# Moving GpSimd's weight scaling, a split and four additions in a two-layer network with attention, experts and a state-space scan

## The reference

```
h = layernorm(x) * (1 + ca) + sa;  x = x + ga * attention(h)      # 8 heads, latent keys, causal
h = layernorm(x) * (1 + cb) + sb;  x = x + gb * experts0(h)       # 8 experts of 64, 2 chosen
h = layernorm(x) * (1 + ca) + sa;  x = x + ga * mixer(h)          # state-space scan, 16 states
h = layernorm(x) * (1 + cb) + sb;  x = x + gb * experts1(h)       # 8 experts of 512, 2 chosen
```

```
xr = h @ in_w + in_b;  x_in, res = split(xr);  xc = silu(conv4(x_in))
proj = xc @ x_proj_w + x_proj_b;  d_raw, Bm, Cm = split(proj)
delta = softplus(d_raw @ dt_w + dt_b)
state[n] = exp(delta * A[n]) * state[n] + (delta * xc) * Bm[n]     # over the tokens
y = sum_n state[n] * Cm[n] + xc * D;   out = (y * silu(res)) @ out_w + out_b
```

## Time and profile before

| | us |
|---|---|
| median of 3 runs | 1392.08 (1386.74 to 1392.71) |
| the profiled execution, its own time | 1389.78 |
| its span, first to last instruction | 1388.0 |
| TensorE busy | 1209.2 (87%) |
| VectorE busy | 1064.1 (77%) |
| ScalarE busy | 851.7 (61%) |
| GpSimd busy | 494.3 (36%) |

### The profile page before, as it was taken

One profiled execution on the slowest core, in us unless ns is written; L12 is line 12 of the kernel. 1 busy time (PEld: TensorE's weight loads), 2 busy tenths in 40 slices (PEclk: granted clock), 3 DMA queues, 4 the chain that ended last, 5 costly groups with the idle time before them and its releaser, 6 DMA issues. The chain is left out here.

```text
span 1388.0 us, 19464 instructions
## 1 busy us (share of the span) xinstructions
PE 1209.2 (87%) x6560; PEld 756.6 (55%) x6560; DVE 1064.1 (77%) x2381; ACT 851.7 (61%) x1600; POOL 494.3 (36%) x309
## 2 busy tenths in 40 slices
PE   5974689988898989989899889989899899889698
PEld 4641155655655556545556465655556556555466
DVE  3757976599867997599866998689975998579722
ACT  2624455587647856489565866479565876469332
POOL 0104930087102950068200961049300871039300
PEclk9985579999999999999999999999999999999789
DMA  6102100020001100020001200021000300011000
GB/s 243 70 16 77 46 8 1 21 102 16 16 16 62 61 16 1 16 92 31 16 9 47 85 0 17 16 77 47 16 1 16 108 16 9 1 62 61 8 1 9
DMA packets 18514, 53.22 MB, mean 38 GB/s; under 512 B 4976, under 2 KB 5864, under 8 KB 18032
## 3 DMA queue, kind: packets, MB, share of 16 engines
q1 hardware_dynamic: 16112, 43.40, 9.6%
q0 software_dynamic: 1296, 4.20, 1.0%
q10 hardware_dynamic: 1008, 4.38, 0.8%
HBM read 45.40 MB, written 2.38 MB: 34 GB/s over the span
## 5 line engine op out<-in xcount | busy, mean ns | idle before, releaser
L1456 DVE TENSOR_TENSOR_SCAN probs_T<-bank,probs_T 128x512 f32<-128x512 f32 x256 | 302.8, 1211 | 1.5
L593 PEld LDWEIGHTS bank<-w_w,hidden 128*128 128x128 f32 x2048 | 247.2, 192 | 77.9 <-issue 68.2
L442 POOL TENSOR_TENSOR probs_T<-step_space,probs_T 128x1024 f32<-128x1024 f32 x120 | 285.7, 2387 | 0.4
L577 PE MATMUL bank<-hT,w_w 128*128 128x512 f32 x512 | 256.7, 615 | 10.9 <-ACT hidden L908 10.1
L593 PE MATMUL bank<-w_w,hidden 128*128 128x128 f32 x2048 | 252.2, 276 | 5.2 <-DVE expert_sum L1149 4.1
L440 POOL TENSOR_TENSOR probs_T<-step_space,probs_T 128x512 f32<-128x512 f32 x16 | 25.1, 1571 | 633.9 <-DVE step_space L1443 633.9
L908 ACT ACTIVATE hidden<-bank,w_b 128x512 f32<-128x512 f32 x256 | 169.9, 686 | 112.4 <-PE bank L577 111.8
L981 ACT ACTIVATE probs<-bank,row_neg 128x128 f32<-128x128 f32 (+3 forms) x256 | 135.3, 530 | 165.4 <-DVE row_neg L1310 148.4
L1053 ACT ACTIVATE bank<-step_space,a_neg 128x512 f32<-128x512 f32 x256 | 167.8, 683 | 58.0 <-DVE probs_T L1456 42.4
L676 PE MATMUL bank<-k_pad,q_lat 128*128 128x512 f32 (+3 forms) x512 | 184.8, 447 | 5.4 <-DMA k_pad<-xc 5.4
L1310 DVE TENSOR_REDUCE row_neg<-bank 128x1 f32<-128x128 f32 (+3 forms) x256 | 122.2, 486 | 78.8 <-PE bank L678 76.9
(11 more groups left out here) (183 smaller groups left out, 1603.5 us busy)
## 6 DMA issues: line engine op xcount, KB each, us to landing
probs_T<-b_rows_dram SPq DMA_DIRECT2D x64, 512.0 KB, 3.7
w_w<-in_w_dram ACTq DMA_DIRECT2D x2, 2048.0 KB, 14.0
k_pad<-xc SPq DMA_DIRECT2D x64, 64.0 KB, 2.0
x_in<-in_x_dram POOLq DMA_DIRECT2D x8, 256.0 KB, 3.3
gate<-gate_rows_dram SPq DMA_DIRECT2D x1, 2048.0 KB, 7.0
out_dram<-x_out POOLq DMA_DIRECT2D x7, 256.0 KB, 2.8
step_space<-in_wmod_dram SPq DMA_DIRECT2D x1, 768.0 KB, 5.3
probs_T<-in_wqT_dram SPq DMA_DIRECT2D x1, 512.0 KB, 4.1
```

What stands on the lines that cost most here:

```text
L442: ins = nc.gpsimd.tensor_tensor(inject[:, n % 3, :, :], u[:], row.unsqueeze(1).to_broadcast([P, DH, T]), ALU.mult)
L577: mm(hid1_bank(n)[:], w["w1"][:, n // C1, n % C1 * P:(n % C1 + 1) * P], hT[3][:], start=True, stop=True).then_inc(hid1_mm.sem, 1)
L593: ins = mm(to[:, t * P:(t + 1) * P], hidden[:, (e * C1 + c) % (2 * C1), t * P:(t + 1) * P], w["w2"][:, e * C1 + c, :], start=(c == 0), sto ...
L1456: v.tensor_tensor_scan(state[:, n % 2, c, :], decay(DH * n + c)[:], inject[:, n % 3, c, :], 0.0, ALU.mult, ALU.add).then_inc(st_ok.sem, 1)
```

## The change

Three things are done. First, GpSimd's four products for a batch are taken apart. Batch 0's stay together where they were. For batch b the scaled `out_w` is made after the first layer norm of iteration b is written and the mixer's output of batch b-1 is done; `w_vo` for batch b+1 follows at once, after the attention output of b; `wprojT` for b+1 follows the second layer norm and the first layer's expert output of b; `out_b` for b+1 follows the addition of the bias of b. The semaphore counts stay the same (`VO, PROJ, BIAS, OUT` are 1 to 4).

Second, on VectorE the last two instructions of the split go ahead of the deltas, and the four additions of expert 1 go between the second delta and the second u.

Third, TensorE's wait for expert 1's additions ahead of expert 2's products is dropped (`e != EARLY_E`); the two use different banks.

```diff
@@ gpsimd
+            def gate_weight(b, to, weight, k):
+                nc.gpsimd.tensor_tensor(to[:], weight[:], gate[:, b:b + 1, k, :].to_broadcast([P, to.shape[1], P]),
+                                        ALU.mult).then_inc(weights_gated.sem, 1)
...
             def gate_weights(b):
 
-                if b == 0:
-                    pool.wait_ge(weights_in, 16 * n_weights)
-                    pool.wait_ge(gates_spread, 16)
-                    pool.wait_ge(setup_a, 3)
-                else:
-                    pool.wait_ge(attn_mm.sem, attn_mm.at(b - 1, 2))
-                    pool.wait_ge(out0_mm.sem, out0_mm.at(b - 1, 1))
-                    pool.wait_ge(bias_added.sem, bias_added.at(b - 1, 1))
-                for to, weight, k in ((gated_vo, w_vo, 0), (gated_proj, w["wprojT"], 1),
-                                      (gated_bias, w["out_b"][:].unsqueeze(1), 2), (gated_out, w["out_w"], 2)):
-                    n = to.shape[1]
-                    if to is gated_out and b > 0:
-                        pool.wait_ge(mix_mm.sem, mix_mm.at(b - 1, 1))
-                    nc.gpsimd.tensor_tensor(to[:], weight if to is gated_bias else weight[:],
-                                            gate[:, b:b + 1, k, :].to_broadcast([P, n, P]), ALU.mult
-                                            ).then_inc(weights_gated.sem, 1)
+                pool.wait_ge(*nth(ln_xn, b, 1))
+                if b > 0:
+                    pool.wait_ge(mix_mm.sem, mix_mm.at(b - 1, 1))
+                    gate_out(b)
+                if b < B - 1:
+                    pool.wait_ge(attn_mm.sem, attn_mm.at(b, 2))
+                    gate_vo(b + 1)
+                    pool.wait_ge(*nth(ln_xn, b, 2))
+                    pool.wait_ge(out0_mm.sem, out0_mm.at(b, 1))
+                    gate_proj(b + 1)
+                    pool.wait_ge(bias_added.sem, bias_added.at(b, 1))
+                    gate_bias(b + 1)
 
             load(0, True)
             load(1)
+            pool.wait_ge(weights_in, 16 * n_weights)
+            pool.wait_ge(gates_spread, 16)
+            pool.wait_ge(setup_a, 3)
+            gate_vo(0)
+            gate_proj(0)
+            gate_bias(0)
+            gate_out(0)
             gate_weights(0)
@@ tensor, out1
-                    elif e >= 1 and not tail:
+                    elif e >= 1 and e != EARLY_E and not tail:
                         pe.wait_ge(out1_add.sem, out1_add.at(b, e * NT + 1))
@@ vector, iteration
-                early(1)
+                link(cp(split[low, :], part[low, :]))
+                tt(split[low, :], part[low, :], split[low, :], ALU.subtract).then_inc(split_ok.sem, 1)
                 for c in range(DH):
...
                     stt(delta[:, c, :], dt_in[:, c, :], 0.0, dt_log[:, c, :], ALU.max, ALU.add).then_inc(delta_ok.sem, 1)
+                    if c == 1:
+                        early(1)
                     dve.wait_ge(delta_ok.sem, delta_ok.at(b, c + 1))
                     tt(u[:, c, :], delta[:, c, :], xc[:, c, :], ALU.mult).then_inc(u_ok.sem, 1)
-                link(cp(split[low, :], part[low, :]))
-                tt(split[low, :], part[low, :], split[low, :], ALU.subtract).then_inc(split_ok.sem, 1)
```

More of the change, by code:

```diff
@@ L232, in build, with gated_weight @@
         weights_gated = signal("weights_gated", 4)
+        VO, PROJ, BIAS, OUT = range(1, 5)
+        def gated_weight(b, which):
+            return weights_gated.sem, weights_gated.at(b, which)
         bias_added = signal("bias_added", 1)
@@ new lines, in gate_vo, with gate_proj, gate_bias, gate_out @@
+            def gate_vo(b):
+                gate_weight(b, gated_vo, w_vo, 0)
+            def gate_proj(b):
+                gate_weight(b, gated_proj, w["wprojT"], 1)
+            def gate_bias(b):
+                gate_weight(b, gated_bias, w["out_b"][:].unsqueeze(1), 2)
+            def gate_out(b):
+                gate_weight(b, gated_out, w["out_w"], 2)
+            def gate_weights(b):
+                pool.wait_ge(*nth(ln_xn, b, 1))
[10 more added lines that the diff above has]
+                    gate_bias(b + 1)
@@ L647, in mixer_out_mm @@
                 pe.wait_ge(z_ok.sem, z_ok.at(b, DH))
-                pe.wait_ge(weights_gated.sem, weights_gated.at(b, 4))
+                pe.wait_ge(*gated_weight(b, OUT))
                 for t in range(NT):
@@ L717, in attention_out @@
                     pe.wait_ge(y_out.sem, y_out.at(b, G + half + 1))
-                    pe.wait_ge(weights_gated.sem, weights_gated.at(b, 1))
+                    pe.wait_ge(*gated_weight(b, VO))
                     for t in range(2 * half, 2 * half + 2):
@@ L779, in out0 @@
                     pe.wait_ge(hid0_gate.sem, hid0_gate.at(b, c + 1))
-                    pe.wait_ge(weights_gated.sem, weights_gated.at(b, 2))
+                    pe.wait_ge(*gated_weight(b, PROJ))
                     for t in range(NT):
@@ L1413, in iteration @@
                 dve.wait_ge(*nth(ln_xn, b, 2))
-                dve.wait_ge(weights_gated.sem, weights_gated.at(b, 3))
+                dve.wait_ge(*gated_weight(b, BIAS))
                 tt(x[:], x[:], gated_bias[:].to_broadcast([P, NT, P]), ALU.add).then_inc(bias_added.sem, 1)
```

## The result

| | before | after |
|---|---|---|
| median, 7 runs each, us | 1389.5 (1386.7 to 1392.7) | 1379.2 (1374.5 to 1382.5) |
| ratio after / before | | 0.9922, 95% interval 0.9905 to 0.9940 |
| span of the profiled execution | 1388.0 | 1379.8 |

The change made the kernel 10.8 us faster (8.3 to 13.2 by the interval). I forecast 13.9 us faster and 1377.0 us, with a range from 1367 to 1385. Direction and range hold. The two terms behind the sum do not: the attention gave more than I wrote, and the start of the scan gave nothing.

What follows compares the result with a forecast made beforehand. No engine alone bounds the kernel: VectorE sets the scan's pace, TensorE's queue and short waits between three engines the attention's. Terms 9.0 + 4.5 + 0.4 = 13.9 us faster gave 1377 us, range 1367 to 1385.

Steps and rivals of the forecast that it cites:

- Part 1, the stall and TensorE's slack: Attention: without VectorE's stalled copy, unit 10's transposes start 1.59 us earlier in batches 2 to 6; 9.0 us in all.
- The rival with the whole stall on the path: Attention: all of VectorE's lost time counts, 19 us, for 1366 us, or 1371 with half the difference; chance 0.16.
- the one with the stall hidden: Attention: the stall cost nothing and only the scan's start pays, giving 1385 us; chance 0.13.
- if another wait follows directly: Attention: lower bound of the 9.0 us term, a gain of nothing, as ScalarE has a backlog behind the stall.
- The covers of the moved products: GpSimd's products fall in three VectorE waits, of 3.45, 3.14 and 3.29 us, and cost nothing there.
- The rule on the ports: Attention: by the skill's rule the copy goes on after one product, some 0.7 us later; the trace shows 2.48 us.
- Part 2, the start of the scan: Scan start: VectorE's new order saves 0.64 us in each of 7 batches, 4.5 us, plus 0.4 in batch 0.
- So the second half of state 1 starts at 610.03 + 0.04 + 0.05 = 610.12: Scan start, batch 3: ScalarE's fourth decay sets this time, against 610.76 before, 0.64 us earlier; delta 0 comes 0.04 later.
- the earlier split does not help it: Scan start: ScalarE's chain from delta 1 to the fourth decay gains nothing, as hidden chunks wait for ScalarE's own GELUs.
- Part 3, TensorE's wait: Ahead of expert 2's products: keeping the wait would cost TensorE about 3 us; dropped, they start as before, cost nothing.
- The total: Whole kernel: 9.0 + 4.5 + 0.4 = 13.9 us faster, taken as 1377 us; chance 0.55.

Runs made afterwards that it cites:

- the added product: Kernel before, with one more GpSimd product of the projection's size, into a spare tile, in batches 1 to 7: ratio 1.0065, 9.0 us slower.
- filled row: Changed kernel, with TensorE making the first row of C eight times more ahead of the one that counts: ratio 0.9884, in a second run 0.9866, against before.
- both edits: Changed kernel, with the split's subtraction behind expert 1's additions and six extra makings of the first row of C: ratio 0.9894 against before.
- moved products alone: Kernel before, with only GpSimd's products moved, VectorE's order and TensorE's wait as before: ratio 0.9901, 13.8 us faster.
- late subtraction: Changed kernel, with the split's subtraction moved behind expert 1's additions, ahead of u1: ratio 0.9913 against before.
- row of C held back: Changed kernel, with TensorE waiting for GpSimd's second injection before the first row of C: ratio 0.9918 against before.
- new order alone: Kernel before, with VectorE's new order ahead of the scan and TensorE's wait dropped, GpSimd's products as before: ratio 0.9998.
- wait kept: Changed kernel, with TensorE's wait for expert 1's additions ahead of expert 2's products restored: ratio 1.0005 against before.

## Why the prediction was right, and where it was not

- **Part 1, the stall and TensorE's slack: right in mechanism, too small in size.** The transposes of unit 10 came where the sum had them, to 0.01 us. The rival with the whole stall on the path (19 us) and the one with the stall hidden both fell; the added product shows that beyond the slack each microsecond counts. The term is 11.5 instead of 9.0, because I took ScalarE's backlog only as a lower bound ("if another wait follows directly"), where it was one more thing that the stall had delayed: it gives 0.34 us more by the router.
- **The covers of the moved products: right.** In batches 1 to 6 the stretches between the attention and the scan changed by 0.01 us at most.
- **The rule on the ports.** The Trainium skill ("SBUF — State Buffer", Who interferes with whom) has the ports held for one instruction. In the kernel before a copy was shut out over three (batches 2 to 6); with gaps of less than 0.1 us it got in behind the first. So the rule holds when there is a gap. Without one, a copy can be shut out over several products, but not always: in batch 7, where it came in the middle of the second product, it got in ahead of the third after 0.92 us, and in batches 1 to 6 it got in ahead of the fourth. What lets it in at a border without a gap is open.
- **Part 2, the start of the scan: the step that failed.** "So the second half of state 1 starts at 610.03 + 0.04 + 0.05 = 610.12" has two faults. The small one is the 0.04: delta 0 came 0.25 us later, not 0.04. The cast of the split began 1.56 us behind `dt_in` where the additions had begun after 1.45, and the subtraction of the split and delta 0 do not overlap (754.62 + 0.68 = 755.30, then 755.33). That leaves 0.38 of 0.64 us, measured in every undisturbed batch. The large one is "the earlier split does not help it": it was not neutral either. The row of C that before lay behind TensorE's idle time, directly ahead of the hidden chunks, went in front of it, and TensorE then stood idle 2.33 us instead of 1.82. In five of seven batches the clock fell around chunks 14 and 15, and these batches lost 0.60 to 1.59 us against the 0.38 of the others, 5.2 us in all. The prediction has no term for the clock and no rival with it: the 1.00 of the earlier trace rows is that of the old order. The expectations that followed took batch 7 for undisturbed; it was not.
- **Part 3, TensorE's wait: right that it must go.** Kept, it leaves TensorE idle for 3.30 us per batch, where I had written about 3. What that costs on the path I had not worked out: 2.6 us per batch against an undisturbed one, of which 1.71 (an estimate) go with the low clock, and 12 us in all against the changed kernel by the ratios.
- **The total** came out within 3.1 us by luck. Two errors have opposite signs: 2.5 us too little in the attention, 7.1 too much in the starts of the scans (4.9 forecast, -2.2 measured). About 1 us then came from the clock at the end of batch 7, which I had not forecast either.

Open is what exactly makes the clock fall. The idle time of TensorE between expert 2's products and hidden chunk 14 (in the last row elsewhere), and the batches with a clock below 1.00 in the 8 us of the start:

| kernel | idle, us | batches of 7 |
|---|---|---|
| filled row (two runs), both edits | 0.6, 0.5 | 0, 0, 0 |
| before; moved products alone | 1.82 | 0; 0 |
| late subtraction | 0.07 + 1.80 | 4 |
| row of C held back | 1.71 + 0.46 (batch 1: 2.52) | 5 |
| changed kernel; new order alone | 2.33 | 5; 3 |
| wait kept | 3.30, ahead of expert 2's products | 7 |

The kernels with 1.82 and with 1.87 us differ little, and yet one has no fall in 14 starts and the other four in seven. In the first, the row and the chunks come behind the idle time, in the other the chunks alone. The runs do not separate these.

## What to carry to other kernels

Price a stall on one engine by the engine that ends last, and then ask once more what backlog the stall leaves, since that goes too. When an edit lets an instruction start earlier, look at the idle time it leaves behind on its own engine: on TensorE an idle stretch of 2.33 us took the two chunks behind it from 1.98 to as much as 3.57 us here, and a few useless matmuls in it were worth more than the edit. GpSimd's products, spread over its program or only spaced by waits on itself, disturbed VectorE less than the same products in one block.

## What I had not expected of the hardware

- A VectorE copy of 0.29 us waited for three GpSimd products in a row (2.48 us), and for four with one more (3.72 us), but only for one (0.81 us, and 1.04 at most) when each product was followed by a gap of 0.07 to 0.08 us.
- TensorE's granted clock went from 2.4 to 1.2 GHz behind idle times of about 2 us in the midst of dense work, in some batches and not in others of the same execution, with the same instructions: 3 of 7 and 5 of 7 starts. Six matmuls of 128x512 took 4.43 instead of 3.03 us in batch 4 of the kernel after. The Trainium skill ("TensorE: Matmul & The Clock Gate", Part 1) describes a clock that follows how busy the array has been; the filled row, which took away the idle time and with it all falls, agrees with it.
- The cost of such a fall depends on when it comes. It was 1.59 us when the clock fell 0.19 us ahead of chunk 14 and 0.60 us when it fell 1.24 us behind its start, each time what chunk 15 ended late.
